# GELU and SiLU straight from ScalarE's tables in three more dense passes of a two-layer kernel

## The reference, cut to what matters

```
x = x + xattn0(layernorm(x), ctx)      # softmax over 512 columns
x = x + ffn0(layernorm(x))             # dense FFN + top-2 of 8 experts, both with GELU (tanh form)
x = x + xattn1(layernorm(x), ctx)      # 16 heads, RoPE, causal softmax
x = x + ffn1(layernorm(x))             # dense FFN with SiLU

# ffn0, dense part: gelu(h @ w_gate) * (h @ w_up) @ w_down      512 -> 2048 -> 512
# ffn0, an expert:  gelu(h @ we_gate) * (h @ we_up) @ we_down   512 ->  256 -> 512
# ffn1:             silu(h @ w_gate) * (h @ w_up) @ w_down      512 -> 2048 -> 512
# gelu(z) = 0.5 z (1 + tanh(0.79788 (z + 0.044715 z^3))),  silu(z) = 0.5 z (1 + tanh(z / 2))
```

## Time and profile before

| | us |
|---|---|
| median of 3 runs | 1904.25 |
| lowest, highest | 1895.87, 1905.53 |
| the profiled execution, its own time | 1901.84 |
| its span, first to last instruction | 1900.1 |
| PE busy | 1708.6 (90%) |
| DVE busy | 1190.2 (63%) |
| ACT busy | 805.2 (42%) |

### The profile page before, as it was taken

One profiled execution on the slowest core, in us unless ns is written; L12 is line 12 of the kernel. 1 busy time (PEld: TensorE's weight loads), 2 busy tenths in 40 slices (PEclk: granted clock), 3 DMA queues, 4 the chain that ended last, 5 costly groups with the idle time before them and its releaser, 6 DMA issues.

```text
span 1900.1 us, 27374 instructions
## 1 busy us (share of the span) xinstructions
PE 1708.6 (90%) x9396; PEld 1351.9 (71%) x9396; DVE 1190.2 (63%) x2583; ACT 805.2 (42%) x1802; POOL 248.8 (13%) x253
## 2 busy tenths in 40 slices
PE   4678899789988998779999999877899999999998
PEld 3467687668988986567667767665776678678887
DVE  5789775365656647985666766799656563553332
ACT  4456552234666643322645554442245462431110
POOL 1225324390000004110000000321100000000000
PEclk7788899899999999889999999899999999999999
DMA  3356669888889886659534415888972546236562
GB/s 107 127 189 223 231 226 354 328 326 323 272 293 321 260 323 237 204 188 319 191 95 133 139 57 178 338 318 306 301 229 79 150 129 216 82 126 203 193 217 89
DMA packets 135464, 409.52 MB, mean 216 GB/s; under 512 B 15136, under 2 KB 29856, under 8 KB 129568
## 3 DMA queue, kind: packets, MB, share of 16 engines
q1 hardware_dynamic: 125200, 372.65, 57.5%
q0 software_dynamic: 10128, 35.13, 4.9%
HBM read 282.95 MB, written 124.78 MB: 215 GB/s over the span
## 4 chain that ended last, share of the span: by engine, by line
PE 60%; DVE 18%; DMA 7%; issue 7%; ACT 4%; POOL 2%; SPq 1%; another core or an unknown queue 0%; POOLq 0%; ACTq 0%; DVEq 0%
PE ps L1178 16%; PE ps L1180 15%; PE ps L1179 15%; PE ps L1326 5%; DMA raw<-in_ffn_w 4%; PE ps L1335 3%; PE ps L1318 2%; DVE gu L1670 2%; POOL xg_dram L1118 2%; DVE act L1655 1%; PE ps L1184 1%; DVE wd L1670 1%; DMA gu<-w_dram 1%; ACT hid L1383 1%; DVE va L1741 1%
## 5 line engine op out<-in xcount | busy, mean ns | idle before, releaser
L1178 PE MATMUL ps<-xT,gu 128*128 128x512 f32 (+1 forms) x1392 | 541.3, 389 | 96.2 <-DVE gu L1670 29.6
L1179 PE MATMUL ps<-xT,gu 128*128 128x512 f32 (+1 forms) x1392 | 517.6, 372 | 0.0
L1180 PE MATMUL ps<-xT,gu 128*128 128x512 f32 (+1 forms) x1392 | 517.0, 371 | 0.0
L1178 PEld LDWEIGHTS ps<-xT,gu 128*128 128x128 f32 x1392 | 273.3, 196 | 156.6 <-issue 55.3
L1180 PEld LDWEIGHTS ps<-xT,gu 128*128 128x128 f32 x1392 | 272.1, 195 | 44.9
L1179 PEld LDWEIGHTS ps<-xT,gu 128*128 128x128 f32 x1392 | 273.4, 196 | 36.8
L1178 PE MATMUL ps<-wd,hid 128*128 128x512 f32 x604 | 249.2, 413 | 17.7 <-DVE acc L1690 5.3
L1180 PE MATMUL ps<-wd,hid 128*128 128x512 f32 x604 | 239.4, 396 | 0.0
L1179 PE MATMUL ps<-wd,hid 128*128 128x512 f32 x604 | 239.3, 396 | 0.0
L1383 ACT ACTIVATE hid<-act 128x512 fp32r<-128x512 f32 (+1 forms) x174 | 100.0, 575 | 265.5 <-DVE act L1655 260.7
L1670 DVE TENSOR_TENSOR gu<-raw,gu 128x512 fp32r<-128x512 f32 x188 | 135.5, 744 | 78.8 <-ACT gu L1399 72.1
(11 more groups left out here) (273 smaller groups left out, 2420.7 us busy)
## 6 DMA issues: line engine op xcount, KB each, us to landing
gu<-w_dram SPq DMA_DIRECT2D x160, 512.0 KB
raw<-in_ffn_w SPq DMA_DIRECT2D x94, 768.0 KB
wd<-w_dram SPq DMA_DIRECT2D x80, 512.0 KB, 5.4
w_dram<-gu SPq DMA_DIRECT2D x32, 1024.0 KB
w_dram<-wd SPq DMA_DIRECT2D x32, 512.0 KB
QT<-q_dram SPq DMA_DIRECT2D x48, 256.0 KB, 5.8
xg_dram<-zt POOLq DMA_DIRECT2D x23, 512.0 KB, 5.4
x<-xg_dram SPq DMA_DIRECT2D x23, 512.0 KB, 5.9
```

Of the source, the lines that this page charges most:

```text
L1178: mm(out_ap, ah, bh, start=start, stop=False)
L1179: mm(out_ap, ah, bl, start=False, stop=False)
L1180: return mm(out_ap, al, bh, start=False, stop=stop)
```

## The change

`mode` names two forms by their function now, and gives the table to more passes. (0,2) goes from the polynomial to the GELU table; (1,0) and (1,3) go from tanh to the SiLU table. (0,3) keeps the polynomial, (1,1) and (1,2) keep tanh: these are the passes beside which the attention's exponentials run. (0,0), (0,1) and the experts had the table already. The planner's costs follow, five of them also for the PE items `logit`, `values`, `norm` and `project`, and `merge` works out all orders anew. Scatter of expert rows, tiles and DMAs stay as they are.

```diff
     def mode(s):
         kind, f, b, _ = MAIN[s]
-        if f == 1:
-            return "silu"
-        return "poly" if kind == "F" and b >= 2 else "gelu"
+        if kind == "F" and (f, b) in ((0, 3), (1, 1), (1, 2)):
+
+            return "tanh" if f else "poly"
+        return "table"
...
         if kind == "mix":
-            return {"gelu": [], "silu": [("DVE", 0.6)], "poly": [("ACT", 0.55), ("DVE", 0.6)]}[mode(a[0])]
+            return {"table": [], "tanh": [("DVE", 0.6)], "poly": [("ACT", 0.55), ("DVE", 0.6)]}[mode(a[0])]
...
-            "bet": [("DVE", 0.75)], "aexp": [("ACT", 0.72)], "resid": [("DVE", 0.85)], "xh": [("POOL", 1.25)], "logit": [("PE", 0.85), ("DVE", 0.1)],
+            "bet": [("DVE", 0.75)], "aexp": [("ACT", 0.72)], "resid": [("DVE", 0.85)], "xh": [("POOL", 1.25)], "logit": [("PE", 0.95), ("DVE", 0.1)],
...
-                    if mode(s) == "gelu":
-                        func(o, z, ACT.Gelu_apprx_tanh).then_inc(free[0], 1)
-                    elif mode(s) == "silu":
+                    if mode(s) == "table":
+                        func(o, z, ACT.Silu if MAIN[s][1] else ACT.Gelu_apprx_tanh).then_inc(free[0], 1)
+                    elif mode(s) == "tanh":
                         func(o, z, ACT.Tanh, scale=0.5).then_inc(tanh_ready, 1)
```

More of the change, by code:

```diff
@@ L271, in steps @@
             "comb": [("DVE", 1.25), ("ACT", 1.3)], "parts": [("DVE", 1.35), ("POOL", 1.3), ("ACT", 0.65)], "final": [("DVE", 2.3)], "qrow": [("ACT", 0.71), ("DVE", 1.3)],
-            "qsum": [("POOL", 1.3)], "qt": [("PE", 0.36), ("ACT", 0.48), ("DVE", 0.6)], "inv": [("DVE", 0.4)], "values": [("PE", 0.36)], "norm": [("PE", 0.1), ("ACT", 0.3), ("DVE", 0.25)],
-            "split": [("ACT", 0.53), ("DVE", 0.6)], "project": [("PE", 2.75), ("DVE", 0.6)], "rown4": [("ACT", 0.71)], "rowt4": [("PE", 0.36), ("ACT", 0.48), ("DVE", 0.6)],
+            "qsum": [("POOL", 1.3)], "qt": [("PE", 0.36), ("ACT", 0.48), ("DVE", 0.6)], "inv": [("DVE", 0.4)], "values": [("PE", 0.47)], "norm": [("PE", 0.22), ("ACT", 0.3), ("DVE", 0.25)],
+            "split": [("ACT", 0.53), ("DVE", 0.6)], "project": [("PE", 2.85), ("DVE", 0.6)], "rown4": [("ACT", 0.71)], "rowt4": [("PE", 0.36), ("ACT", 0.48), ("DVE", 0.6)],
             "rn2": [("DVE", 1.5), ("PE", 2.0), ("ACT", 0.5)], "zero": [("POOL", 0.75)]}.get(kind, [])
@@ L406, in leaves_bank @@
         kind, *a = item
-        return {"sim": ("scale", *a), "scores": ("exp", *a), "values": ("norm", *a[0:2]), "gate0": ("gate" if mode(a[0]) == "gelu" else "mix", a[0]) if kind == "gate0" else None,
+        return {"sim": ("scale", *a), "scores": ("exp", *a), "values": ("norm", *a[0:2]), "gate0": ("gate" if mode(a[0]) == "table" else "mix", a[0]) if kind == "gate0" else None,
                 "up0": ("mult", *a), "downs": ("down", *a[0:2])}.get(kind, item)
@@ L783, in two_layers @@
         POLY = {s: n + 1 for n, s in enumerate(s for s in range(len(MAIN)) if mode(s) == "poly")}
-        TANH = {s: n + 1 for n, s in enumerate(s for s in range(len(MAIN)) if mode(s) != "gelu")}
+        TANH = {s: n + 1 for n, s in enumerate(s for s in range(len(MAIN)) if mode(s) != "table")}
         def last_down(g):
@@ L809, in half @@
         def half(s):
-            return 1.0 if mode(s) == "gelu" else 0.5
+            return 1.0 if mode(s) == "table" else 0.5
         def unit(b, n):
```

## The result

| | before | after |
|---|---|---|
| median, 20 runs each on one chip (us) | 1904.64 | 1897.76 |
| lowest, highest | 1895.87, 1912.7 | 1889.85, 1908.81 |
| profiled execution, its own time | 1901.84 | 1899.77 |

The ratio is 0.9966, with a 95% interval of 0.9953 to 0.9979. So the change gives 0.34%, some 7 us: less than the 0.5% called "no change" ahead of it, of 39 us forecast, and outside the range of 1843 to 1885.

The account below looks back on a forecast made before the run. PE was taken to bound the full passes, DVE (0,2) and (1,0). The terms -32 - 9 + 0 + 2 + 0 = -39 us gave 1862.8 us, with 2.4 us added 1865 us for the median; range 1843 to 1885.

Parts of the forecast that it names:

- Pass (0,2), -32: GELU table in (0,2) frees DVE: 29 us in the mid-work stretch and 2.5 in plain tiles, ends -27 and -45.
- The share: In (0,2)'s mid-work stretch DVE stays 86.5% busy, so 21.6 us less DVE work gains 25 us.
- The hops: In (0,2), 7.7 us of waits of `mix` and `cube` for ACT vanish; the stretch takes 122.7 us, gain 29.
- rival B: (0,2) and (1,0) fall to PE's pace at full clock, -45 and -12 us: about 1848 us; chance 0.12.
- The plain tiles: In (0,2)'s four tiles outside the mid work, three intervals of 6.27 us become 5.44, a gain of 2.5 us.
- Pass (1,0), -9: SiLU table in (1,0) removes `mix`, 8.2 us of DVE over twelve tiles: 9 us gained, ends 0 and -12.
- Pass (1,3), 0: SiLU table in (1,3) saves 11 us of DVE, but PE's own work hides it: 0 us gained.
- Table loads, +2: Five more ACT table loads of 1.28 us; only the two in (0,0) cost time, +2 us, ends 0 and 2.6.
- The orders, 0 with ends of 8: In (0,0) and (0,1) side work moves later; one PE wait may go, shrink or be added: 0, ends -8 and +8.
- A: DVE's time doesn't hold (0,2), the mid work's latency does; only plain tiles gain: about 1904 us; chance 0.05.
- C: (1,0) is held by DMA, so only -32 + 2 us remain: about 1874 us; chance 0.15.
- D: New order in (0,0) and (0,1) delays scatter and key load, stopping ACT, DVE, PE: slower, about 1915 us; chance 0.04.

Follow-up runs that it names:

- experiment 4: GELU table in (0,2) alone, all else as in the kernel before: 1886.99 us, ratio 0.9908.
- experiment 1: Table functions in (0,2), (1,0) and (1,3), with planner, costs and orders of the kernel before: 1879.46 us, ratio 0.9868.
- experiment 3: Changed kernel with the planner's old PE costs of `logit`, `values`, `norm` and `project`, orders worked out anew: 1879.68 us, ratio 0.988.
- experiment 7: The changed kernel run once more, nothing altered: 1898.64 us, ratio 0.9977.
- experiment 6: Changed kernel with the old PE cost of `logit`, but the new ones of `values`, `norm` and `project`: 1891.51 us, ratio 0.9942.
- experiment 2: Kernel before with its old functions, only the planner's four PE costs set to the new ones: 1907.68 us, ratio 1.0024.

## Why the prediction was wrong, step by step

**What bounds the kernel: right.** PE in the full passes, DVE in (0,2) and (1,0). No pass that was full got shorter by more than 2 us.

**Pass (0,2), -32, ends -27 and -45: the mechanism right, the size not.** It gave -17.5 (experiment 4), -16.6 in the pass. The amount of DVE work was right: 1.80 us a tile, and the pass went from 143 to 117 us of it. Three terms of the sum fell:

- The share. I divided the 21.6 us by DVE's share, 25 us. In before's orders DVE lost 19.2 us in that stretch and the time 18. An idle time that doesn't come from the removed instructions doesn't shrink with them.
- The hops, 4 us more. They went, and a wait for PE of 8.6 us came, nearly all of it at the ends of the stretch, where a tile goes at the pace of PE and the weights and not of DVE. The twelve tiles are 98 us of PE and some 3 for queries; I took this for free room below 122.7, though the same text says against rival B that two engines so evenly loaded don't run without waits. That argument belonged into the sum, as a price. The weights, for which PE waits 6.2 us in this stretch now, had no term at all.
- The plain tiles, -2.5. I took 5.44 us from (1,3), where DMA's share is 0.49; in the plain tiles of (0,2) it was 1.02 before the change. In (0,2) they are 6.3 us apart still, of which the last two after are

```profile
865.10 0.60 ACT L1370 ACTIVATE act<-ps 128x512 f32<-128x512 f32 x1 [0.84 <-PE ps L1181]
871.35 0.60 ACT L1370 ACTIVATE act<-ps 128x512 f32<-128x512 f32 x1 [2.18 <-PE ps L1181]
```

The changed kernel's new order makes it no better. Its stretches, plain, mid work, plain:

```profile
709.00:733.00 24.00, 23.23 (x95) 18.48 (x94) 4.14 (x6) 5.36 (x9) 3.68 (x4) 0.94 1.01 404
733.00:857.00 124.00, 99.74 (x400) 78.67 (x399) 107.41 (x283) 36.62 (x82) 32.46 (x28) 0.90 0.67 230
857.00:874.00 17.00, 16.47 (x77) 13.34 (x76) 5.42 (x9) 4.25 (x7) 1.59 (x2) 1.00 0.98 361
```

The mid work takes 124 us, close to the 122.7 of the sum, with DVE at 86.6%. But it holds ten tiles and not twelve, for the planner packs it closer. The other six take 41 us, at a DMA share of 1.01 and 0.98. What is saved inside the stretch is time only if the stretch still covers the same tiles.

**Pass (1,0), -9: right,** as far as the functions go: -7.6 for (1,0), (1,3) and their loads together (experiments 1 and 4, with overlapping intervals). The pass has 178.4 us, where some 175 were asked.

**Pass (1,3), 0: right.** 147 to 149 us in all traces, whether DVE is busy 37 us in it or 48.

**Table loads, +2: too much, within its ends.** The trace has 16, of 1.28 us, and had 11 before (15 and 10 leave out the one at 0.8 us): five more, as foreseen. With two more of them (0,0) lasts 192.4 us, against 195.1; it begins 3.2 us later and ends at 280.7 us, against 280.1. One of them, on ACT in order of time:

```profile
146.27 1.51 ACT L1453 ACTIVATE xn<-x,s_nm,s_rs 128x512 f32<-128x512 f32 x2
147.80 1.28 ACT L1479 ACT_TABLE_LOAD   x1
149.09 0.73 ACT L1479 ACTIVATE va<-va,a_nm 128x512 f32<-128x512 f32 x1
```

**The orders, 0 with ends of 8: the step that failed most.** They cost 18 us (experiments 3 and 7). I looked at the text of the orders where the routing stands, found that the side work had moved by a tile or two, and priced one wait of that size. I didn't look at (1,0) and (1,1), though the change touched the costs of `values`, `norm` and `project`, which stand just there, and 12 of the 18 us came from those three (experiment 6). "0" stood there without a row for these passes. "PE's full passes have no idle time to gain" was true, and the wrong question: they have some to lose. (1,1) had 4.0 us of idle time and has 8.7, beside work that moved into it.

**The rivals.** A, that DVE doesn't hold (0,2), is refuted: -17.5 us from DVE work alone. B didn't come; even with (0,2) at 147 us PE was idle 18 us in it. Against C speak the 7.6 us, and (1,0) with 179.5 us in experiment 1 against 185.5 in 4. D had the right kind of cause, a new order that costs nearly what the functions give. It had it in the wrong place for the most part, and its 40 us were too many. (0,0) is not longer at all, (0,1) and the experts by 12 us in a stage where one order differs by more between executions, and the chain that D told, scatter, keys, squares, isn't what showed there.

**What remains open.** How a cost of 0.1 us more for `logit` makes 6 us, and where: only the wait for `acc` points to it, and experiment 2 speaks against the place. Most of the 12 us of the other three, of which one gap explains 3.4. And why the same costs take 18 us with the new functions and 5 with the old: the old ones have DVE as the bound in (0,2) and (1,0) anyway, which may hide a part, but no run isolates that.

## What to carry to other kernels

A change in a planner's costs is a change of its own. Price it apart from the functions it comes with, at every item whose cost it touches, and try the functions with the old orders first: here that was a kernel faster by 1.3%, not by 0.3%. Where the freed engine meets another one loaded nearly as much, count one us of time at most for each us of work removed (18 for 19.2 here), nothing for idle time that would vanish, and take the pace of a plain tile from a pass with the same DMA share. And where two executions of one program differ by 10 us in a stage, one trace of each kernel doesn't show which stage a change of 6 us lies in.

## What the runs showed of the hardware

*The DMA queues as a bound.* The plain tiles of (0,2) run at a DMA share of 1.01 with 404 GB/s and are 5.9 to 6.4 us apart (8.2 where twelve down matmuls of the experts lie between), with PE waiting up to 0.6 us for weights before a gate product. In experiment 3 PE waits 3.3 us for them in 694 to 718 us, at a share of 1.02 and 417 GB/s, and two tiles are 7.0 us apart. At a share of 0.49, in (1,3), tiles are 5.44 us apart. Before the change the share was the same 1.02 at 405 GB/s, but PE's wait there was put down to `mix`, for the polynomial took as long.

*DVE and POOL side by side.* `parts` on DVE (L1877) and the addition on POOL (L1165), both on 128x512 fp32 in SBUF, in the changed kernel's (0,2), start and duration in us:

```profile
812.85 0.74 DVE L1877 SCALAR_TENSOR_TENSOR yb<-ya,p_r,postB 128x512 f32<-128x512 f32 x1
813.51 0.74 DVE L1876 SCALAR_TENSOR_TENSOR dn<-dn,p_r,postB 128x512 f32<-128x512 f32 x1
813.67 1.73 POOL L1165 TENSOR_TENSOR dn<-dn,yb 128x512 f32<-128x512 f32 x1 [1.75 <-DVE yb L1877]
814.18 1.78 DVE L1877 SCALAR_TENSOR_TENSOR yb<-ya,p_r,postB 128x512 f32<-128x512 f32 x1
...
816.04 1.27 POOL L1165 TENSOR_TENSOR dn<-dn,yb 128x512 f32<-128x512 f32 x1 [0.63 <-DVE yb L1877]
```

Alone, DVE's step takes 0.74 us, and POOL's last one here 1.27. The two that meet take 1.78 and 1.73. All four such meetings of L1877 in this pass took DVE 1.74 to 2.12 us, some 4 us in all that no count of instructions shows. The Trainium skill ("SBUF — State Buffer", SBUF: two separate sides) says that a DVE operation with two inputs in SBUF and a GpSimd operation that reads SBUF take a shared pair of ports as an exclusive lock, and that the later one waits. The trace agrees in both directions. DVE's L1877 starts while POOL is at work and ends 0.56 us after it, most of its own 0.74. And POOL's step starts 0.16 us behind DVE's L1876, another step with two inputs in SBUF: it takes 0.46 us more than 1.27, about what that one (to 814.25 us) had left.
